# Recurrence: mixes, feeds and turns of a token tile as 64x64 tensor tiles, in four pieces placed behind different steps

## What is computed

```
x = tokens * rsqrt(mean(tokens^2) + 1e-4) * norm_w      # per token, then split into 16 heads of 16
state = tanh(einsum('bhs,hst->bht', state, tanh(a)) + einsum('bhd,hds->bhs', x_t, b))   # 64 wide, step by step
mixed = einsum('bhs,hsd->bhd', state, c) + skip * x_t
out = tokens + mixed.reshape(B, T, 256) @ w_out.T + b_out
```

## Time and profile before

| | us |
|---|---|
| median of three executions | 2248.2 |
| the profiled execution | 2250.94 |
| its span, first to last instruction | 2249.2 |
| mean granted TensorE clock | 0.991 of 2.4 GHz |
| recurrence, start of the first and of the last tanh | 1531.0, 2051.8 |

### The profile page before, as it was taken

How to read it: one execution, slowest core, us unless ns; L and a number is a source line. 1 busy time by engine, 2 the same in 40 slices (tenths; PEclk the granted TensorE clock), 3 DMA queues, 4 the chain that set the end, 5 groups by cost and what they waited for, 6 DMA issues and landing times.

```text
span 2249.2 us, 90212 instructions
## 1 busy us (share of the span) xinstructions
PE 2192.8 (97%) x36480; PEld 1535.0 (68%) x36480; DVE 1708.7 (76%) x4852; ACT 1061.6 (47%) x2707; POOL 1195.4 (53%) x1680
## 2 busy tenths in 40 slices
PE   9999999999999999999999999998999999999997
PEld 5566565556555555556777777777888888886775
DVE  5788888888887777769999999994555555555997
ACT  4655665656666665552222222222444444443444
POOL 4555555655655555536666666664444444442334
PEclk9999999999999999999999999998999999999999
DMA  4111111211211111111211011100011111111232
GB/s 150 58 50 56 67 63 62 67 58 58 67 67 58 67 59 57 56 46 31 68 33 33 30 33 33 40 24 29 28 33 37 33 33 33 37 49 37 89 94 76
DMA packets 101633, 117.81 MB, mean 52 GB/s; under 512 B 10672, under 2 KB 80080, under 8 KB 101456
## 3 DMA queue, kind: packets, MB, share of 16 engines
q1 hardware_dynamic: 101456, 115.44, 15.8%
HBM read 48.29 MB, written 33.55 MB: 36 GB/s over the span
## 4 chain that ended last, share of the span: by engine, by line
PE 92%; DVE 4%; issue 1%; ACT 1%; POOL 0%; DMA 0%; DVEq 0%; ACTq 0%; SPq 0%; POOLq 0%
PE ps_state L1731 10%; PE ps_down L1373 7%; PE ps_gate L1366 7%; PE ps_up L1366 7%; PE ps_near L812 6%; PE ps_far L592 5%; PE ps_near L584 5%; PE ps_far L584 4%; PE ps_near L592 3%; PE ps_far L627 3%; PE ps_far L611 3%; PE ps_far L604 3%; PE ps_state L1762 3%; PE ps_state L1734 2%; PE ps_r L2136 2%; PE ps_v L2147 2%
## 5 line engine op out<-in xcount | busy, mean ns | idle before, releaser
L1613 ACT ACTIVATE r_state<-ps_state 128x64 f32<-128x64 f32 x1024 | 229.4, 224 | 291.5 <-PE ps_state L1734 286.6
L1731 PE MATMUL ps_state<-r_state,later_pairs_a 64*64 64x32 f32 x8192 | 334.9, 219 | 19.7 <-ACT r_state L1613 12.5
L1731 PEld LDWEIGHTS ps_state<-r_state,later_pairs_a 64*64 64x64 f32 x8192 | 295.2, 135 | 80.2 <-issue 60.4
L1734 PE MATMUL ps_state<-r_state,later_pairs_a 64*64 64x32 f32 x8192 | 335.7, 220 | 1.9 <-issue 1.7
L480 DVE CUSTOM_DVE_ANT_0 ps_near<-ps_near,mask 128x512 f32<-128x512 f32 (+1 forms) x512 | 270.6, 590 | 84.3 <-PE ps_near L584 84.3
L340 POOL TENSOR_SCALAR_AFFINE_SELECT probsT<-probsT 128x512 f32<-128x512 f32 x256 | 160.4, 639 | 267.3 <-ACT probsT L460 167.9
L1734 PEld LDWEIGHTS ps_state<-r_state,later_pairs_a 64*64 64x64 f32 x8192 | 289.4, 135 | 2.4 <-issue 2.4
L480 DVE CUSTOM_DVE_ANT_0 ps_far<-ps_far,mask 128x384 f32<-128x384 f32 (+1 forms) x512 | 198.4, 459 | 33.6 <-PE ps_far L584 32.5
L1256 POOL TENSOR_TENSOR f_fp<-f_rounded,f_scale 128x960 f32<-128x960 f32 (+2 forms) x67 | 117.4, 1752 | 162.1 <-DVE f_rounded L1345 162.1
L1278 ACT ACTIVATE f_silu<-ps_gate 128x704 f32<-128x704 f32 x64 | 48.6, 759 | 285.7 <-PE ps_gate L1366 285.7
L592 PE MATMUL ps_far<-Q,K 32*128 32x256 f32 (+2 forms) x1536 | 182.0, 419 | 1.2 <-ACT probsT L457 0.5
(11 more groups left out here) (216 smaller groups left out, 5388.0 us busy)
## 6 DMA issues: line engine op xcount, KB each, us to landing
q_swap<-q_sin SPq DMA_DIRECT2D x128, 128.0 KB, 2.1
k_swap<-k_sin SPq DMA_DIRECT2D x128, 128.0 KB, 2.1
xT<-in_xT_dram SPq DMA_DIRECT2D x16, 512.0 KB, 3.6
xtok<-in_x_dram SPq DMA_DIRECT2D x16, 512.0 KB, 3.8
x_rows<-x SPq DMA_DIRECT2D x16, 512.0 KB, 2.9
f_x<-x_rows SPq DMA_DIRECT2D x64, 128.0 KB, 2.1
x_rows<-f_x SPq DMA_DIRECT2D x64, 128.0 KB, 1.8
r_x<-x_rows SPq DMA_DIRECT2D x64, 128.0 KB, 2.0
```

The costliest lines, as they stand in the source:

```text
L1613: nc.scalar.activation(state[:, j % 2, banks, :, t, 0, :], sums[j % 2][:, banks, :, now], ACT.Tanh).then_inc(state_ready[t], 1)
L1731: nc.tensor.matmul(sums[j % 2][half(v), stays, c, now], A[half(v), 3 * q, c, :], last[half(v), stays, c, :], start=False, stop=True, skip_ ...
L1734: out = nc.tensor.matmul(sums[j % 2][half(1 - v), changes, c, now], A[half(v), 3 * q + 1 + was, c, :], last[half(v), changes, c, :], start ...
```

## The change

- **Mixes.** `mix` takes a piece: chunk piece // 2, and for even pieces the banks that stay (4 matmuls, 128 columns), for odd ones the banks that change (8 matmuls, 64 columns). Weights are 64x64, one half of the partitions at a time, so that a chunk's mix comes as two partial sums in two banks (`MIX`). VectorE adds the skip and one bank, drains, and adds the other bank.
- **Feeds.** `inputs` takes a piece as well: pieces 0 and 1 feed the banks that stay, of chunk 0 and 1 (4 matmuls, 128 columns each), pieces 2 and 3 those that change (8 matmuls, 64 columns each). `pairs_b` holds b twice with zeros, so that 64 rows serve where 32 did.
- **Turn.** In place of two transposes of 128x128 it is 8 matmuls of 64x64 channels with 64 columns of the identity, into two banks, and `turned` scales in four instructions of 64 columns in place of two of 128. It also waits for the second mix to have left its banks (`outs_ready`).
- **Slots.** Mixes in 0, 1, 2, 3; projections in 5 and 8; the turn in 6; feeds in 9, 11, 12, 13. The wait for `z_added` moves from the first feed to the third piece. In the first tile the turn is in 8 and the feeds in 11 to 14. The very first turn keeps the two transposes.

The diff, without the sizes of `pairs_b` and `pairs_c` and the host's filling of them:

```diff
@@ -1441,7 +1441,10 @@
     SIDES = 2
     BANKS = 4
-    TURN, MIX, OUT = 1, (1, 3), (2, 0)
+    MIX, OUT, TURN = ((1, 3), (0, 2)), (1, 3), (0, 2)
+    FIRST_TURN = 3
     def sb(name, shape, dt=F32):
         return memory.enter_context(nc.sbuf_tensor("r_" + name, shape, dt))
@@ -1636,8 +1639,6 @@
         def turned(i, j):
-            bank = MIX[1] if isinstance(i, int) and i == -1 else TURN
             at = j % 2 if isinstance(i, int) and i == -1 else (j + 1) % 2
             dve.wait_ge(x_turned, i + 2)
             if later(i, 1, 2):
@@ -1645,7 +1646,9 @@
                 dve.wait_ge(inputs_in, i)
                 dve.wait_ge(outs_ready, 2 * i + 2)
             for c in range(CC):
-                out = nc.vector.tensor_scalar(xT[:, (j + 1) % 2, c, :], room[at][:, bank, c * P:(c + 1) * P], norm_w[:, c:c + 1], None, ALU.mult)
+                for r in range(2):
+                    bank, columns = (FIRST_TURN, slice(c * P + r * STATE, c * P + (r + 1) * STATE)) if isinstance(i, int) and i == -1 else (TURN[r], half(c))
+                    out = nc.vector.tensor_scalar(xT[:, (j + 1) % 2, c, half(r)], room[at][:, bank, columns], norm_w[:, c:c + 1], None, ALU.mult)
             out.then_inc(xT_ready, 1)
         def normalise(i, j):
@@ -1672,8 +1675,10 @@
                     if later(i, -1, 2):
                         dve.wait_ge(out_full, i - 1)
-                    nc.vector.scalar_tensor_tensor(outs[:, s, c, :], xT[:, s, c, :], skip[:, c:c + 1], room[s][:, MIX[c], 0:P],
-                                                   ALU.mult, ALU.add).then_inc(outs_ready, 1)
+                    nc.vector.scalar_tensor_tensor(outs[:, s, c, :], xT[:, s, c, :], skip[:, c:c + 1], room[s][:, MIX[c][0], 0:P],
+                                                   ALU.mult, ALU.add)
+                    dve.drain()
+                    nc.vector.tensor_tensor(outs[:, s, c, :], outs[:, s, c, :], room[s][:, MIX[c][1], 0:P], ALU.add).then_inc(outs_ready, 1)
             if exists(i, 1):
                 turned(i, j)
             if exists(i, 2):
@@ -1736,21 +1741,21 @@
                                            start=False, stop=True, skip_group_check=True)
             out.then_inc(summed[q], 1)
-        def inputs(j, c):
-            s = (j + 1) % 2
-            for parity in range(2):
+        def inputs(j, piece):
+            s, c, odd = (j + 1) % 2, piece % CC, piece // CC
+            for parity in range(1 + odd):
                 for v in range(2):
-                    for bank in range(BANKS):
-                        rows = slice(32 * bank, 32 * bank + 32)
-                        xT_now = xT[rows, s, c, :]
-                        if bank % 2:
-                            out = nc.tensor.matmul(steps_of(sums[s][half(v ^ parity), bank, c, :], parity), B[rows, 2 * c + v, :], steps_of(xT_now, parity),
+                    for r in range(2):
+                        bank, weights_of, xT_now = 2 * r + odd, B[half(r), odd, 2 * c + v, :], xT[half(r), s, c, :]
+                        if odd:
+                            out = nc.tensor.matmul(steps_of(sums[s][half(v ^ parity), bank, c, :], parity), weights_of, steps_of(xT_now, parity),
                                                    start=(c == 0 and parity == 0), stop=False, skip_group_check=True)
-                        elif parity == 0:
-                            nc.tensor.matmul(sums[s][half(v), bank, c, :], B[rows, 2 * c + v, :], xT_now,
-                                             start=(c == 0), stop=False, skip_group_check=True)
+                        else:
+                            out = nc.tensor.matmul(sums[s][half(v), bank, c, :], weights_of, xT_now,
+                                                   start=(c == 0), stop=False, skip_group_check=True)
             return out
         def project(j, c, states):
@@ -1770,27 +1775,43 @@
             for n in range(times):
                 nc.tensor.matmul(room[(j + 1) % 2][:, bank, :], quiet[:, 0:P], quiet[:], start=start, stop=True, skip_group_check=True)
-        def mix(j, c):
-            s = (j - 1) % 2
-            for parity in range(2):
-                for bank in range(BANKS):
-                    into = room[s][32 * bank:32 * bank + 32, MIX[c], 0:P]
-                    if bank % 2:
-                        out = nc.tensor.matmul(steps_of(into, parity), C[:, 3 * (bank // 2) + 1 + parity, c, :], state[:, s, bank, c, parity::2, 0, :],
-                                               start=(parity == 0), stop=True, skip_group_check=True)
-                    elif parity == 0:
-                        nc.tensor.matmul(into, C[:, 3 * (bank // 2), c, :], state[:, s, bank, c, :, 0, :], start=True, stop=True)
-            return out
-        MIXES, PROJECTS, TURNS, FEEDS = (1, 3), (5, 9), 7, (13, 15)
+        def mix(j, piece):
+            s, c, changes = (j - 1) % 2, piece // 2, piece % 2
+            for n in (1, 2) if changes else (0,):
+                for cols in range(2):
+                    for r in range(2):
+                        into = room[s][half(cols), MIX[c][r], 0:P]
+                        weights_of = C[half(r), 3 * cols + n, c, :]
+                        if n == 0:
+                            out = nc.tensor.matmul(into, weights_of, state[half(r), s, 2 * cols, c, :, 0, :], start=True, stop=False, skip_group_check=True)
+                        else:
+                            out = nc.tensor.matmul(steps_of(into, n - 1), weights_of, state[half(r), s, 2 * cols + 1, c, n - 1::2, 0, :],
+                                                   start=False, stop=True, skip_group_check=True)
+            if changes:
+                out.then_inc(mix_full, 1)
+        MIXES, PROJECTS, TURNS, FEEDS = (0, 1, 2, 3), (5, 8), 6, (9, 11, 12, 13)
+        FIRST_TURNS, FIRST_FEEDS = 8, (11, 12, 13, 14)
         LAST_PROJECTS, MIXING = (5, 7), 11
-        def turn(j, at, bank):
+        def first_turn():
             for c in range(CC):
-                out = nc.tensor.transpose(room[at][:, bank, c * P:(c + 1) * P], xn[:, (j + 1) % 2, c * P:(c + 1) * P], ident[:])
+                out = nc.tensor.transpose(room[1][:, FIRST_TURN, c * P:(c + 1) * P], xn[:, 0, c * P:(c + 1) * P], ident[:])
+            out.then_inc(x_turned, 1)
+        def turn(j):
+            at = (j + 1) % 2
+            for c in range(CC):
+                for v in range(2):
+                    for r in range(2):
+                        channels = xn[half(r), at, c * P + v * STATE:c * P + (v + 1) * STATE]
+                        out = nc.tensor.matmul(room[at][half(v), TURN[r], half(c)], channels, ident[half(r), half(r)], start=True, stop=True, skip_group_check=True)
             out.then_inc(x_turned, 1)
         def step(i, j):
@@ -1799,34 +1820,40 @@
             states = [held(2 * i + 1), held(2 * i + 2)]
             first, last = (isinstance(i, int) and i == n for n in (0, TILES - 1))
             projects = LAST_PROJECTS if last else PROJECTS
+            turns, feeds = (FIRST_TURNS, FIRST_FEEDS) if first else (TURNS, FEEDS)
             def slots(t):
                 for q in range(SIDES):
+                    at = SIDES * t + q
                     if exists(i, 0):
+                        if at == 0:
+                            await_count(inputs_in, this_tile)
                         recur(j, t, q, states)
-                    at = SIDES * t + q
                     if at in MIXES and not first:
                         if at == MIXES[0]:
                             for side in range(SIDES):
                                 await_count(state_ready[STEPS - 1], states[side])
-                        mix(j, MIXES.index(at)).then_inc(mix_full, 1)
-                    if at == TURNS and exists(i, 1):
+                        mix(j, MIXES.index(at))
+                    if at == turns and exists(i, 1):
                         await_count(xn_ready, next_tile)
-                        turn(j, (j + 1) % 2, TURN)
+                        if first:
+                            pe.wait_ge(*fed[1])
+                        await_count(outs_ready, states[1])
+                        turn(j)
                     if at in projects and not first:
                         project(j, projects.index(at), states)
                     if at == MIXING and last:
                         pe.wait_ge(z_added, TILES)
                         mixing.to(0)
-                    if at in FEEDS and exists(i, 1):
-                        c = FEEDS.index(at)
-                        if c == 0:
+                    if at in feeds and exists(i, 1):
+                        piece = feeds.index(at)
+                        if piece == 0:
                             await_count(xT_ready, next_tile)
+                        if piece == CC:
                             await_count(z_added, this_tile)
-                            if first:
-                                pe.wait_ge(*fed[1])
-                        out = inputs(j, c)
```

(22 more changed lines are left out.)

2 lines of the change are left out of this document (1 added, 1 removed).

## The result

| | median, us | lowest to highest | ratio, 95% interval |
|---|---|---|---|
| before | 2248.55 | 2247.14 to 2252.18 | |
| changed | 2556.97 | 2532.68 to 2565.15 | 1.1345 (1.1305 to 1.1385) |

The change makes the kernel 13.4% slower, 308 us, where 2250.8 was forecast. The profiled execution took 2565.15 us. Its page: the span; the granted clock in 40 slices of 64 us; the instruction queue; and the chain that ended last, by engine.

What follows compares the result with a forecast made beforehand. It took TensorE's work and the loop of state, matmul and tanh as close limits, neither alone pricing the change. 62 x 0.0 a tile plus 2.6 on 2248.2 gave 2250.8 us, own range 2243 to 2259, whole range 2232 to 2268.

Steps and rivals of the forecast that it cites:

- Rival D: Recurrence loop body too long for instruction memory: a stop in each of 31 passes, +31 to +84 us, 2280 to 2335; chance 0.05.
- Once: Costs outside the repeated tiles: one more instruction block +1.5, adds behind the last state +0.8, first scaling +0.3; +2.6 us.
- A: The forecast's main case: the step sum holds within 0.13 a tile, 2243 to 2259 us; chance 0.45.
- The price of the pieces: TensorE's new mix, feed and turn pieces: 0.25 us each without shape-change drains; its own work falls some 0.3 a tile.
- What lies between: Recurrence steps 0 to 7 of a tile, side 0's recur to recur: sum 7.68 us, same as now, freed time becoming waits.
- The branch: Branch back at the loop's end, adding 0.16 us to every second tile: no change, 0.1 either way.
- VectorE: Second add 0.35 us, four scalings 0.9; outs ready 0.15 before the turn, first feed just covered.
- B: Rival: TensorE's freed time is kept in the recurrence, 0.2 to 0.4 us a tile gained, 2233 us; chance 0.29.
- C: Rival: side 1 decides, pieces cost 0.29 us, six in the chain add 0.22 a tile, 2264 us; chance 0.21.

Runs made afterwards that it cites:

- e1: The changed kernel with 20 one-column matmuls (40 instructions) ahead of the loop, so its body touches seven blocks: 2268.25 us, ratio 1.0082.
- e5: The changed kernel with all new pieces in odd slots, last feed in 15, and 20 one-column matmuls ahead of the loop: 2255.25 us, ratio 1.0030.
- e11: e5 with the feeds moved to slots 11, 11, 13, 13, mixes in 1, 1, 3, 3: 2240.49 us, ratio 0.9944.
- e9: The kernel before with only the wait for `inputs_in` added at slot 0, ahead of the recur: 2278.80 us, ratio 1.0113.
- e3: The kernel before with 39 one-column matmuls in each looped tile, body 1595 instructions touching seven blocks: 2659.47 us, ratio 1.1822.
- e2: The changed kernel with 10 one-column matmuls ahead of the loop, body still touching eight blocks: 2402.8 us, median of four from 2285.91 to 2539.41.
- e10: The changed kernel with mixes in old form (slots 1, 3), 64x64 turn in 7 and feeds in 11, 11, 13, 13: 2235.30 us, ratio 0.9929.
- e12: e10 with 20 one-column matmuls ahead of the recurrence's first step, so its body starts at 5 in a block: 2232.00 us, ratio 0.9921.
- e6: The changed kernel with only the turn in 64x64 tiles (slot 7), mixes and feeds in old form and slots: 2283.44 us, ratio 1.0143.

## Why the prediction was wrong, by its steps

**Rival D, "The loop no longer fits".** This is the step that failed, in its chance and in its size: the forecast puts nothing for it. It counted 1384 matmul and load records now and 1536 later, "six held", against room for 2048 instructions, by which it fits, and gave 0.05. With the waits and the branch the bodies are 1439 and 1595 instructions, and the old one touches seven blocks and not six. What counts is how many blocks the body touches, and so where it begins; and the 28 instructions that the change adds to the first tile, which the prediction counted under "Once", moved that from 193 to 221. With 1595 instructions a body that starts at 221 touches eight blocks, one that starts at 5 (e1) seven; the first costs 308 us and the second 18.

The size was put at 1 to 2.7 us a pass, from one stop in the first pass. One stop at a border was mostly of that size (0.6 to 2.8, once 3.5; 4.8 to 5.3 at the branch), but a long pass has up to seven stops, with nine fetches for the eight blocks of the body. The sign that the prediction named for D, packets on the instruction queue between 1600 and 2000 us, is the one that showed it. A long pass costs 20 to 23 us over one of 16.0, and the next 1.5 to 2.7 more, as the granted clock, which fell in the pass with the stops, is not yet back (0.72 and 0.83 in the windows above, 1.00 in the clean pass). The 13 long passes are 273 us over 16.0 each and the 13 behind them 24; together 297, and the spans of the changed kernel and of e1 differ by 297.6 (2563.3 and 2265.7).

The Trainium skill (Runtime: NRT & Kernel Launch, Instruction fetch mechanics) says that a taken branch out of the current window of two pages forces a fetch, and that crossing a border is mostly hidden. The runs agree that the branch is where it begins (the 5.18 us); they differ on the two pages, since seven blocks loop without a fetch in e1 and e5 to e11, and on "mostly hidden", with stops of 0.6 to 2.8 us at borders in a long pass.

D is not all of the miss. e1, with D out of the way, takes 2268.25: 17 us above the forecast, beyond A's own range (2243 to 2259) and at the very end of the whole one (2232 to 2268). Those 17 us are in the steps below.

**The price of the pieces** was right. The pieces of a tile after, without the branch's disturbance (start, us from first start to last end, records):

```profile
1910.55 0.45 PE L1788 MATMUL ps_state<-r_state,later_pairs_c 64*64 64x128 f32 x8
...
1910.98 0.22 PE L1736 MATMUL ps_state<-r_state,later_pairs_a 64*64 64x32 f32 x1
1910.99 0.47 PE L1790 MATMUL ps_state<-r_state,later_pairs_c 64*64 64x64 f32 x16
...
1913.45 0.47 PE L1814 MATMUL ps_state<-kept_ident,r_xn 64*64 64x64 f32 x16
...
1915.84 0.46 PE L1757 MATMUL ps_state<-r_xT,later_pairs_b 64*64 64x128 f32 x8
...
1916.32 0.47 PE L1754 MATMUL ps_state<-r_xT,later_pairs_b 64*64 64x64 f32 x16
```

Between the starts of neighbours lie 0.44 to 0.48, a recur of 0.20 and a piece of 0.25, as forecast, with none of the 0.15 of a change of shape: from the last recur record to the second mix it is 0.01.

**What lies between**, step by step, was right too. Every second tanh of a tile without a branch, side 0's:

```profile
1918.94 0.23 ACT L1616 ACTIVATE r_state<-ps_state 128x64 f32<-128x64 f32 x1 [0.82 <-PE ps_state L1739]
...
1919.97 0.22 ACT L1616 ACTIVATE r_state<-ps_state 128x64 f32<-128x64 f32 x1 [0.19 <-PE ps_state L1739]
...
1920.89 0.23 ACT L1616 ACTIVATE r_state<-ps_state 128x64 f32<-128x64 f32 x1 [0.24 <-PE ps_state L1739]
...
1921.95 0.23 ACT L1616 ACTIVATE r_state<-ps_state 128x64 f32<-128x64 f32 x1 [0.44 <-PE ps_state L1739]
...
1922.81 0.22 ACT L1616 ACTIVATE r_state<-ps_state 128x64 f32<-128x64 f32 x1 [0.15 <-PE ps_state L1739]
...
1923.95 0.22 ACT L1616 ACTIVATE r_state<-ps_state 128x64 f32<-128x64 f32 x1 [0.25 <-PE ps_state L1739]
...
1924.82 0.22 ACT L1616 ACTIVATE r_state<-ps_state 128x64 f32<-128x64 f32 x1 [0.25 <-PE ps_state L1739]
...
1925.74 0.23 ACT L1616 ACTIVATE r_state<-ps_state 128x64 f32<-128x64 f32 x1 [0.23 <-PE ps_state L1739]
...
1926.68 0.22 ACT L1616 ACTIVATE r_state<-ps_state 128x64 f32<-128x64 f32 x1 [0.32 <-PE ps_state L1739]
```

The steps are 1.03, 0.92, 1.06, 0.86, 1.14, 0.87, 0.92 and 0.94, in sum 7.74; forecast 1.06, 0.93, 1.06, 0.82, 1.14, 0.86, 0.95 and 0.86, in sum 7.68. Seven are within 0.04 of the forecast, and the last is off by 0.08. In e1 these tiles take 7.74 to 7.81. That side 1's waits would eat TensorE's freed 0.3 was the central claim, and e11 shows it from the other side: in odd slots the same pieces give 7.38 to 7.43.

**The branch, "no change, 0.1 either way"**, was mis-sized. In e1 it adds 0.44 to every second tile (8.22 and 7.78), where it added 0.16. From the last record ahead of the branch to the first behind it there were 0.40, and in e1 there are 0.71. Before, the feed in slot 15 stood between side 1's last recur and the branch, and I take it that it hid a part of the branch; now nothing stands there, and side 1's last recur is itself late. No run takes the two apart. 30 x 0.28 for the branch and 60 x 0.1 for the tiles are 14.4; the 30 passes of e1 measure 13.3 over before, and with 1.7 ahead of them and 1.5 behind that is the 16.5 by which the spans differ (17.7 by the medians).

**VectorE** was right as cover, with its terms a little high. Outs and second add of the second chunk, and the four scalings:

```profile
1912.46 0.35 DVE L1678 SCALAR_TENSOR_TENSOR r_outs<-r_xT,later_recurrence_columns,ps_state 128x128 f32<-128x128 f32 x1 [0.23 <-PE ps_state L1790]
1912.88 0.29 DVE L1681 TENSOR_TENSOR r_outs<-r_outs,ps_state 128x128 f32<-128x128 f32 x1
1913.99 0.86 DVE L1651 TENSOR_SCALAR r_xT<-ps_state,later_recurrence_columns 128x64 f32<-128x64 f32 x4 [0.82 <-PE ps_state L1814]
```

The second add takes 0.29 and not 0.35, the scalings 0.86 and not 0.9, and the first feed did not wait for them. Rivals B and C did not decide. e1's 0.47 a pass over before is close to C's 0.44, but it comes mostly from the branch and from the last step, and not from pieces of 0.29.

**What it left out** is the wait for `inputs_in` at slot 0. In the changed kernel's own slots it cost nothing; with the feeds where they stood before it costs 0.9 a pass (e9), more than all the pieces save.

## What to carry to other kernels

When an edit lengthens a loop, count TensorE's instructions in the body and in what stands ahead of it, and see in how many blocks of 256 the body falls from where it starts; here seven ran free, all but one pass of e3, and eight cost up to 13%, and code outside the loop decided. Whether the same holds on another engine no run here shows. A profile shows it as issue in the chain, packets on the instruction queue in mid-loop, and passes of very different length. Read a suspicious stage pass by pass before you explain its mean, and read every wait that a diff adds, since one of them can hold the gain of all the rest; the version that covers it (turn and feeds in 64x64 tiles, feeds in 11, 11, 13, 13, mixes as they were) is 0.7 to 0.8% faster than the kernel before.

## What the runs showed of the hardware that was not expected

- A loop body that touches eight blocks has two ways to run, with fetches and without, and changes between them within one execution: 26 clean passes in a row in e2, and no more than two without a fetch between long ones in the changed kernel.
- Matmuls of one column on a constant can be dear. In e3, 78 of them made a pass 13.4 us longer. At most 4 us of this are their own, since their records start 0.05 apart (an estimate, 78 x 0.05); the rest goes with TensorE's granted clock, which stood at 0.50 for nearly the whole loop though its busy share rose to all 400 us of the window. Whether the filler or the stops of the first pass took the clock down is open.
- The branch back costs 0.67 to 0.72 from the last record ahead of it to the first behind it when nothing stands in between (e10, e11, e12). A block border in the first recurs behind it adds 0.18 (e10 against e12).
- A recur that waits for TensorE's own last matmul starts 0.67 to 0.79 behind the start of that matmul's last record (e5 to e9), where it is 0.15 without the wait and without a branch, and 0.40 with the branch (before).
- The clock can fall without a fetch. e6's passes are 16.45, but four of the 30 are 19.1 to 19.2: in one tile of each the granted clock is at its lower level for some 7 us, a mean of 0.65 over the 9 us below (columns as in the earlier trace rows). TensorE was busy for 8.24 of 9 us ahead of it; e9, with passes as long, kept 1.00 between 1600 and 2000 us, and what tells the two apart is open.

```profile
1711.00:1720.00 9.00, 8.24 (x425) 7.21 (x416) 4.94 (x17) 3.89 (x18) 3.81 (x10) 1.00 0.09 29
1722.00:1731.00 9.00, 8.79 (x312) 7.60 (x313) 3.84 (x13) 3.08 (x14) 1.53 (x4) 0.65 0.09 29
1731.00:1739.00 8.00, 7.28 (x360) 6.35 (x360) 4.00 (x14) 3.45 (x17) 3.08 (x9) 1.00 0.10 33
```
